# Sixteen-head attention kernel: output sums on VectorE instead of ScalarE and GpSimd, with value loads in quarters

## What is computed

```python
xn = _layernorm(x)
k, q, v = W_K xn, W_Q xn, W_V xn             # per head, 2048 x 128
attn = softmax(mask(k q) / sqrt(128))        # 2048 x 2048, causal
out  = sum over heads of W_O (attn v)        # 2048 x 256
x + out + W2 fwht(silu(W1 xn) * (W3 xn))
```

## Time and profile before

| | |
|---|---|
| median of three runs | 1408.76 us |
| the profiled execution | 1413.05 us, span 1411.0 us |
| mean granted TensorE clock, share of full speed | 0.984 |
| TensorE matmul busy | 1342.5 us, 95% |
| VectorE, ScalarE, GpSimd busy | 67%, 67%, 68% |
| DMA queues' share of 16 engines' span | 74.6% |
| a head (start to start) | about 70.7 us |

### The profile page before, as it was taken

The page is one execution under the profiler, slowest core; times in us unless marked ns, Lnnn a source line. Parts: engine busy times, 40 slices in busy tenths (PEclk is TensorE's granted clock), DMA queues, the critical chain, the costliest instruction groups (busy, mean ns, idle before and its releaser), DMA issues.

```text
span 1411.0 us, 26546 instructions
## 1 busy us (share of the span) xinstructions
PE 1342.5 (95%) x8138; PEld 1198.1 (85%) x8138; DVE 938.8 (67%) x2131; ACT 950.2 (67%) x1926; POOL 961.2 (68%) x634
## 2 busy tenths in 40 slices
PE   6999999999999999999999999999999999999987
PEld 5788888788888888888888888888888888888876
DVE  6544200767767777777777777787777777777763
ACT  4332344677768777778776877787778777877774
POOL 6111000277869787879787978797879787978794
PEclk9999999999999999999999999999999999999999
DMA  4200166797888889888888898888898889898883
GB/s 151 71 1 0 37 193 189 205 293 252 263 271 258 287 259 288 259 285 259 281 258 270 272 283 269 286 266 287 259 286 264 287 262 290 256 287 263 278 252 98
DMA packets 275741, 330.72 MB, mean 234 GB/s; under 512 B 62576, under 2 KB 248048, under 8 KB 271344
## 3 DMA queue, kind: packets, MB, share of 16 engines
q1 hardware_dynamic: 275696, 330.19, 74.6%
HBM read 170.85 MB, written 159.25 MB: 234 GB/s over the span
## 4 chain that ended last, share of the span: by engine, by line
POOL 41%; issue 29%; PE 17%; DMA 4%; SPq 3%; DVE 3%; ACT 2%; POOLq 1%; ACTq 0%; DVEq 0%
POOL pt_lo L462 28%; POOL acc L453 9%; PE ps L970 6%; PE ps L971 6%; PE ps L972 6%; SPq L353 3%; DMA scratch<-raw 3%; POOL v_lo L467 3%; DMA pt_lo<-scratch 1%; POOL wqk_lo L442 1%; DVE raw L902 1%; ACT raw L655 1%; POOLq L461 1%; DVE had L892 0%; DVE pt_lo L913 0%
## 5 line engine op out<-in xcount | busy, mean ns | idle before, releaser
L462 POOL TENSOR_TENSOR pt_lo<-pt_lo,pt_hi 128x896 fp32r<-128x896 f32 (+2 forms) x378 | 651.8, 1756 | 140.1 <-ACT pt_hi L662 140.0
L655 ACT ACTIVATE raw<-ps,had 128x1024 f32<-128x1024 f32 (+7 forms) x384 | 329.4, 867 | 163.6 <-DVE had L895 133.7
L902 DVE STREAM_TRANSPOSE raw<-raw 128x2048 f32<-128x2048 f32 (+3 forms) x252 | 317.0, 1292 | 105.5 <-ACT raw L655 103.2
L970 PE MATMUL ps<-pt_hi,v_hi 128*128 128x256 f32 (+1 forms) x1152 | 327.1, 284 | 35.1 <-POOL v_lo L467 27.4
L971 PE MATMUL ps<-pt_lo,v_hi 128*128 128x256 f32 (+1 forms) x1152 | 333.2, 289 | 0.0
L972 PE MATMUL ps<-pt_hi,v_lo 128*128 128x256 f32 (+1 forms) x1152 | 331.0, 287 | 0.0
L662 ACT CAST pt_hi<-pt_lo 128x896 fp32r<-128x896 f32 (+2 forms) x378 | 284.5, 818 | 35.4 <-DMA pt_lo<-scratch 35.1
L892 DVE TENSOR_REDUCE had<-ps 128x1 f32<-128x1024 f32 (+1 forms) x256 | 237.4, 947 | 46.9 <-PE ps L972 46.7
L970 PEld LDWEIGHTS ps<-pt_hi,v_hi 128*128 128x128 f32 x1152 | 223.2, 194 | 46.0 <-POOL v_lo L467 30.6
L970 PE MATMUL ps<-k_hi,q_hi 128*128 128x512 f32 (+3 forms) x640 | 235.7, 368 | 7.0 <-DVE k_lo L866 5.9
L971 PE MATMUL ps<-k_lo,q_hi 128*128 128x512 f32 (+3 forms) x640 | 233.8, 365 | 0.0
(11 more groups left out here) (113 smaller groups left out, 2222.6 us busy)
## 6 DMA issues: line engine op xcount, KB each, us to landing
v_next<-all_values SPq DMA_DIRECT2D x16, 1024.0 KB, 5.4
scratch<-raw SPq DMA_DIRECT2D x64, 256.0 KB, 5.6
pt_lo<-scratch SPq DMA_DIRECT2D x16, 1024.0 KB, 5.4
scratch<-raw SPq DMA_DIRECT2D x64, 240.0 KB, 5.0
pt_lo<-scratch SPq DMA_DIRECT2D x16, 960.0 KB, 5.9
scratch<-raw SPq DMA_DIRECT2D x64, 224.0 KB, 5.2
pt_lo<-scratch SPq DMA_DIRECT2D x16, 896.0 KB, 4.7
scratch<-raw SPq DMA_DIRECT2D x64, 208.0 KB, 4.7
```

The costliest lines, as they stand in the source:

```text
L462: pool.tensor_tensor(lo, lo.bitcast(F32), hi.bitcast(F32), ALU.subtract).then_inc(pt_lo_done, 1)
L655: act.activation(to, scores, ACT.Exp, bias=neg_max[:, j:j + 1], accum_out=row_part[:, j, e % 2:e % 2 + 1]).then_inc(exped, 1)
L902: dve.transpose(v, v).then_inc(blocked, 1)
L970: pe.matmul(dst, a[0], b[0], start=start, stop=False, skip_group_check=True)
```

## The change

- VectorE's new `output` does the scaling and the addition in one instruction per tile (two per z): `acc = psum * row_rcp + acc`. ScalarE's `output`, GpSimd's `add` and `share` go. Big outputs stand at the end of odd steps, small ones behind the transposes of even steps. TensorE's waits on `shared` become waits on `out_added`.
- VectorE's `z_to_lo` of small sums moves behind the first reduction of `maxima`.
- ScalarE rounds value quarters 0 and 1 at the start of step 4, GpSimd between the second and third piece of step 3.
- `bring_v` is in quarters: 3 and 2 in step 6, 0 in step 7, 1 in step 0 of their own head.
- In step 7 TensorE projects K quarter 2 ahead of `output` of z 2, and ScalarE rounds it, and the small sum, ahead of the probabilities. In the other odd steps the small sum stays between pieces 0 and 1.

```diff
+    V_NEXT = {6: (3, 2), 7: (0,)}
...
-            def bring_v(h):
-                wait(sp, v_lo_done, QUARTERS * h)
-                sp.dma_start(v_next[:, :], all_values[h].rearrange("p i d -> p (i d)")).then_inc(v_moved, 16)
+            def bring_v(h, b):
+                wait(sp, v_lo_done, v_count(h - 1, b))
+                sp.dma_start(v_next[:, b * BANK:(b + 1) * BANK],
+                             all_values[h][:, b * PER_Q:(b + 1) * PER_Q, :].rearrange("p i d -> p (i d)")
+                             ).then_inc(v_moved[b], 16)
...
-                    if s == 5 and h + 1 < HEADS:
-                        bring_v(h + 1)
+                    for b in V_NEXT.get(s, ()) if h + 1 < HEADS else ():
+                        bring_v(h + 1, b)
+                    if s == 0 and h > 0:
+                        bring_v(h, V_ITEMS[-1])
...
-            def add(h, z):
-                c = Z_ORDER[z]
-                pool.wait_ge(shared, z_count(h, z))
-                pool.tensor_tensor(acc[:, 2 * c:2 * c + 2, :], share[:, z % 2, :, :],
-                                   acc[:, 2 * c:2 * c + 2, :], ALU.add).then_inc(out_added, 1)
...
                     if not (first and s < 2) and not over:
-                        for n in range(3):
-                            p_to_lo(hh, ss, n)
+                        p_to_lo(hh, ss, 0)
+                        p_to_lo(hh, ss, 1)
+                    if s == 3 and not over:
+                        for b in V_AT[4]:
+                            v_to_lo(h, b)
+                    if not (first and s < 2) and not over:
+                        p_to_lo(hh, ss, 2)
...
-                ins = act.activation(share[:, z % 2, t, :], z_bank(z, t * D, (t + 1) * D), ACT.Copy,
-                                     scale=row_rcp[:, j:j + 1])
...
-                    if s == 3 and not over:
-                        v_to_hi(h, 2)
+                    for b in V_AT[s] if s in (3, 4) and not over else []:
+                        v_to_hi(h, b)
...
+                    here = not (first and s < 2) and not over
+                    if here and s != 7:
                         p_to_hi(hh, ss, 0)
-                    if s in (1, 3, 5) and not absent(Z_SMALL[s][0]):
-                        z_to_hi(h + Z_SMALL[s][0], Z_SMALL[s][1])
-                    if not (first and s < 2) and not over:
-                        p_to_hi(hh, ss, 1)
-                        p_to_hi(hh, ss, 2)
                     if s == 7 and more:
                         kq_to_hi(h, ("K", 2))
+                    if s in Z_SMALL and not absent(Z_SMALL[s][0]):
+                        z_to_hi(h + Z_SMALL[s][0], Z_SMALL[s][1])
+                    if here:
+                        for n in range(3 if s == 7 else 2):
+                            p_to_hi(hh, ss, n if s == 7 else n + 1)
...
                         dve.tensor_reduce(bank_max[:, j, i:i + 1], scores, AX_X, ALU.max).then_inc(maxed, 1)
+                    if i == 0 and z is not None:
+                        z_to_lo(*z)
...
+            def output(h, z):
+                c = Z_ORDER[z]
+                dve.wait_ge(rcp_done, z_count(h, z))
+                dve.wait_ge(wo_product, z_count(h, z))
+                wait(dve, out_added, z_count(h, z) - 1)
+                for t in range(2):
+                    j = 2 * c + t
+                    ins = dve.scalar_tensor_tensor(
+                        out=acc[:, j, :], in0=z_bank(z, t * D, (t + 1) * D), scalar=row_rcp[:, j:j + 1],
+                        in1=acc[:, j, :], op0=ALU.mult, op1=ALU.add)
+                ins.then_inc(out_added, 1)
...
                         transpose_blocks(h, s, 1)
+                    if s in O_SMALL and not absent(O_SMALL[s][0]):
+                        output(h + O_SMALL[s][0], O_SMALL[s][1])
                     if s < 2 and not over:
                         kq_to_lo(h, ("Q", s + 1))
...
+                    if s in O_BIG and not absent(O_BIG[s][0]):
+                        output(h + O_BIG[s][0], O_BIG[s][1])
...
-                    wait(pe, shared, z_count(h, z) - 2)
+                    wait(pe, out_added, z_count(h, z) - 2)
...
+                    if s == 7 and more:
+                        project_kq(h, ("K", 2))
                     if s in O_BIG and not absent(O_BIG[s][0]):
                         output(h + O_BIG[s][0], O_BIG[s][1])
-                    if s == 7 and more:
-                        project_kq(h, ("K", 2))
```

More of the change, by code:

```diff
@@ L243, in attention_ffn_kernel @@
         v_projected, v_copied, v_stored = sem("v_projected"), sem("v_copied"), [sem("v_stored0"), sem("v_stored1")]
-        v_moved = sem("v_moved")
+        v_moved = [sem(f"v_moved{b}") for b in range(QUARTERS)]
         late_projected, late_copied = sem("late_projected"), sem("late_copied")
@@ L472, in period @@
                 for s in range(5 if over else STEPS):
[L473 to L478, removed]
                     if s == 2 and more and not over:
                         split_qk(h + 1)
-                    for b in [] if over else V_AT.get(s, []):
+                    for b in [] if over or s == 4 else V_AT.get(s, []):
                         v_to_lo(h, b)
@@ L714, in period @@
                         exponential(h, s, 2)
-                    if s in O_SMALL and not absent(O_SMALL[s][0]):
-                        output(h + O_SMALL[s][0], O_SMALL[s][1])
                     if s < 2 and not over:
@@ L727, in period @@
                         kq_to_hi(h, (("Q", 3), ("Q", 0), ("K", 1))[s - 5])
-                    for b in [] if over or s == 3 else V_AT.get(s, []):
-                        v_to_hi(h, b)
+                    if s == 0 and not over:
+                        v_to_hi(h, V_ITEMS[0])
                     if first and s < 4:
@@ L871, in kq_to_lo, with maxima @@
                                              op1=ALU.subtract).then_inc(proj_lo, 1)
-            def maxima(h, s, small):
+            def maxima(h, s, small, z=None):
                 j = row_of(s, small)
@@ L929, in period @@
                 for s in range(5 if over else STEPS):
+                    z = None
                     if s in O_SMALL and not absent(O_SMALL[s][0]):
-                        z_to_lo(h + O_SMALL[s][0], O_SMALL[s][1])
+                        z = h + O_SMALL[s][0], O_SMALL[s][1]
                     if not over:
-                        maxima(h, s, 0)
+                        maxima(h, s, 0, z)
                         maxima(h, s, 1)
+                    elif z is not None:
+                        z_to_lo(*z)
                     if s % 2 == 0 and not (first and s == 0) and not (over and s > 0):
```

19 lines of the change are left out of this document (5 added, 14 removed).

## The result

The changed kernel takes **1419.91 us**, the median of five runs (1416.93 to 1424.12), against 1408.76 us (five runs in the same comparison): a ratio of **1.0069, 95% interval 1.0043 to 1.0094**. It is slower by about 10 us; 1388 was forecast, with a range of 1361 to 1417. The profiled execution took 1419.28 us (span 1417.5) against 1413.05 (1411.0).

What follows compares the result with a forecast made beforehand. TensorE was taken as the bound, its matmuls filling 95% of the span. Waits removed less added (-7), clock (-11) and the end (-3.3) gave -21: 1392 for the profiled execution, 1388 as median, range 1361 to 1417.

Steps and rivals of the forecast that it cites:

- Removed waits: TensorE's waits on values (30 us), K (8.5) and ScalarE's outputs (2.8) go, 41 us in sum.
- Rival B: New waits don't come, additions fall into VectorE's idle time; SP's queue caps the gain at 33 us: 1362, chance 0.17.
- New waits on sums: TensorE waits for z_lo behind VectorE's added work, 2.25 us a head over 15 heads: 34 us.
- The forecast's 0.85: z 5's output in step 2: TensorE starts at 631.4, 0.85 us late, behind VectorE's big output and first reduction.
- z 3: Small sum in step 0: K quarter 2 coming 0.8 us sooner pays for the pair; no new wait, otherwise 0.5.
- The pair: VectorE's two output instructions per z hold back what is behind them by 0.66 us; range nothing to 0.84.
- z 7 and z 1: Small sums in steps 4 and 6: z_lo ends after TensorE asks, a new wait of 0.7 us each.
- Clock: No new wait reaches 1.87 us, so slow stretches go: six times 1.4 and 2.8, at most 11 us gained.
- 1.8 fits into 2.4: SP's queue, step 0: the value quarter's 0.45 issue plus 1.35 landing fits z 0's margin of 0.84 plus 1.55.
- C: Rival, slower: value quarter 1 in step 0 makes z 0 1.25 us late a head, 19 us: 1418, chance 0.17.
- The end: Last output on one engine (0.84 and 1.26 become 0.75), z 3's rounding not behind a DMA (1.90): 3.3 us gained.
- The prediction's mark: Sign to look for: VectorE's outputs take 0.40 to 0.42 us for each of 256 columns.

Runs made afterwards that it cites:

- values_only: Kernel before, with value quarters 0 and 1 rounded where the change has them and z 5's addition moved to the start of step 3: ratio 0.9986.
- values_k: Kernel before, with value quarters 0 and 1 rounded as in the change, K quarter 2 projected one output earlier and rounded ahead of step 7's probabilities: ratio 0.9980.
- before_no_load: Kernel before, without the value loads of heads 1 to 15 (each head uses head 0's values): ratio to the kernel before 0.9803.
- no_step0_quarter: Changed kernel, but value quarter 1 is loaded in step 7 behind quarter 0 instead of in step 0: ratio to the kernel before 0.9982.
- one_load: Changed kernel, but a head's values come in one transfer of 1 MB in step 5 again: ratio to the kernel before 0.9993.

## Why the prediction was wrong

**Removed waits: right in the place, wrong in the worth.** 30 us for values and 8.5 for K were forecast; the balance shows 29.7 and 8.9 gone. That the 41 us would come off the time in full was the step that failed. The prediction read them as losses that stand alone. values_only shows that they don't: take the value wait away, and 28.4 us stand at K. values_k takes both away and gains at most 0.43% of 3.5%. That TensorE waits in these places for the way of the rows (VectorE's transposes, SP's store and load, ScalarE, GpSimd) is the reading that fits ScalarE's wait for rows, 77.6 us against 30.8; shown is that the value loads in the queue are a part of it (before_no_load, 2%), and the rest is argued. Rival B had a cap of this kind ("SP's queue has only 32.9 us of slack"), but the forecast did not carry it over.

**New waits on sums: 34 us forecast, 49.5 measured.** The forecast's 0.85 is from start to start, which is about 0.16 us more than a row's wait (the last matmul's 0.28 less the usual 0.12 to the next). Measured that way, a head has in the median 1.33 us for z 5, 0.92 for z 7, 0.78 for z 1 and 0.17 for z 3, against 0.85, 0.7, 0.7 and nothing. That is 3.20 where 2.25 was forecast, or 14 of the 15.5 us; the rest are longer waits in some heads.
- Half of it is z 5. The pair was put at 0.66 from additions of `ps` and `acc`; it takes 0.77 to the next start, and 0.86 in all. And VectorE comes to the pair later than thought: its rounding of `q_lo` ahead of it starts 1.33 us behind the first scores of step 2, where it was 0.82 before. 0.1 had been allowed for that.
- z 7 and z 1 were forecast as the end of `z_lo` less the time at which TensorE asks. From there to TensorE's start it is another 0.06 us (719.33 to 719.39 in a head shown below).
- z 3 was to be paid for by the earlier K quarter 2; it falls short by 0.17.

**A wait not thought of: 5.7 us.** TensorE now waits for VectorE before it projects K quarter 2, about 0.2 us by the row and 0.3 from start to start in a head (timeline, step 7 of one):

```profile
606.88 0.50 PE L968 MATMUL ps<-xt_hi,wqk_hi 128*128 128x512 f32 x1 [0.16 <-DVE k_lo L841]
```

K quarter 2 is now projected one output earlier, directly behind the weighted sum, and that output no longer covers the subtraction of K quarter 1. The prediction counted that it comes earlier and not what it comes earlier than.

**Clock: right in size, in part by luck.** 11 us forecast, 10.6 measured; mean granted clock 0.994 against 0.984. The prediction missed one slow stretch of the kernel before, at 359.5 us. It follows a wait on a rounded sum that is not in the last head:

```profile
358.01 0.38 PE L970 MATMUL ps<-wo_hi,z_hi 128*128 128x256 f32 x1 [1.81 <-DVE z_lo L906]
```

So there was more to win than it counted, and the shortest wait before a slow stretch was 1.81 us, not 1.87. Against that, the changed kernel has slow stretches at 720.6 and 1403.3 us that were to be gone.

**SP's queue: the failed margin.** "1.8 fits into 2.4" went wrong on both sides. The 1.8 put a quarter's way at 5.4 / 4 = 1.35 us; in the changed kernel a quarter lands 5.2 us after its issue. And the 2.4 looked at z 0 alone. In the head behind the one shown above, an exponential of step 3 has to wait for a store of the queue. It starts 2.79 us ahead of the first scores of step 4, not 3.45 as in the head shown; VectorE's transposes, its reduction and `z_lo` follow:

```profile
712.00 1.12 ACT L650 ACTIVATE raw<-ps,had 128x1024 f32<-128x1024 f32 x1 [0.56 <-DMA scratch<-raw]
714.02 2.51 DVE L879 STREAM_TRANSPOSE raw<-raw 128x1664 f32<-128x1664 f32 x2 [1.55 <-ACT raw L650]
718.92 0.41 DVE L883 TENSOR_TENSOR z_lo<-ps,z_hi 128x256 fp32r<-128x256 f32 x1
```

TensorE then stands 1.41 us for z 7's sum in place of 0.75, 0.54 us for z 0's probabilities, and the clock falls. no_step0_quarter prices the quarter's place at 0.87%. C had the place, and 19 us at z 0; 12 were measured, and only a part of them at z 0. C's time of 1418 is near the 1419.91 measured, but that nearness is chance: it has too much for the quarter, too little for the sums, all of the removed waits as gained, and no gain by the clock.

**The end: 3.3 us forecast.** From TensorE's last output (1405.87 before, 1413.67 after) to the end of the span it is 5.1 and 3.8 us: 1.3 gained, just what one engine in place of two was put at (0.84 + 1.26 - 0.75 = 1.35). The other 1.9 did not come: z 3's wait behind the DMA in step 0 is gone, but the weighted sum behind that output now waits 1.48 us for `pt_lo` at 1390.81, where it did not wait before, and the two last waits on rounded sums are 1.86 and 1.35 us instead of 1.09 and 0.98.

**The sum.** From 1392 to 1419.3 are 27 us. By the balance the sums' waits hold 15.5 of them, the K projection 5.7, the removed waits 2.4 (38.6 of 41), the small gaps 2.3, the end 2.0; that is 28, and terms under 1 us take the rest back. This is bookkeeping: the removed waits have only 2.4 here because the time stands under other names, and by values_k it would not have come off without the new waits either. The quarter in step 0 is inside these terms too: it shows in longer, irregular waits (`z_lo` 48.1 us against 44.1 in one_load, `pt_lo` 3.8 against 1.1). From z 5's output in one head to that in the next it is 70.9 us in the changed kernel where nothing disturbs it and up to 74.2 where something does; in one_load it is 70.6 to 71.2.

## What to carry to other kernels

A wait of the busiest engine is a place, not a price: before it is counted as a gain, remove only its cause and see whether it comes back at the next stop. When one queue carries both a round trip through DRAM on which engines wait and bulk loads that nobody waits for, the step in which a load is issued can be worth more than the load's size. The same holds for a wait that a change adds. Work put ahead of a rounding on which the busiest engine waits shows up in its waits each time, however idle its own engine is on average; but what it costs depends on what else holds the kernel, here from 0.1% beside a megabyte in step 5 to 2.3% without loads.

## What the runs showed of the hardware

VectorE's scaled addition (PSUM by a column of factors, plus SBUF, 256 columns) took 464 ns, against 0.42 us for the plain addition of the earlier trace rows, and two of them 0.86 us. The prediction's mark was 0.40 to 0.42.

The clock fell behind a wait shorter than any that it had fallen behind in the attention stretch before (timeline and window of the changed kernel):

```profile
719.39 0.39 PE L968 MATMUL ps<-wo_hi,z_hi 128*128 128x256 f32 x1 [1.41 <-DVE z_lo L883]
```
```profile
720.60:724.00 3.40, 3.10 (x14) 3.11 (x15) 2.05 (x9) 3.36 (x8) 3.40 (x3) 0.50 0.73 245
```

The prediction had 1.87 us as the shortest such wait (it was 1.81), and 1.33 without a fall. The waits of 1.16 to 1.24 us, one in nearly every head, were followed by the full clock, and so was one of 1.48 us at 377.34. So length alone doesn't decide here. A second wait of 0.54 us stood 1.5 us behind the one of 1.41, at the start of the slow stretch. values_k has a pair with two short waits, and a slow stretch behind it:

```profile
918.50 0.39 PE L978 MATMUL ps<-wo_hi,z_hi 128*128 128x256 f32 x1 [0.72 <-DVE z_lo L914]
...
920.20 0.39 PE L978 MATMUL ps<-pt_hi,v_hi 128*128 128x256 f32 x1 [0.71 <-ACT aux L691]
```
```profile
920.50:923.90 3.40, 3.40 (x18) 3.40 (x17) 2.35 (x9) 3.40 (x9) 3.40 (x3) 0.50 0.85 276
```

What part the second wait of such a pair has was not tried.
